# Attention with the causal mask of single-head score tiles added by VectorE instead of TensorE

## The reference

```python
att = jnp.einsum('bhqd,bhkd->bhqk', q, k) * scale
causal = jnp.tril(jnp.ones((T, T), bool))
att = jnp.where(causal[None, None], att, -jnp.inf)
y = jnp.einsum('bhqk,bhkd->bhqd', jax.nn.softmax(att, axis=-1), v)
qc, kc, vc = ...                     # the same heads against 64 context keys
y = y + jnp.einsum('bhqk,bhkd->bhqd', jax.nn.softmax(attc, axis=-1), vc)
```

## Time and profile before

| what | us |
|---|---|
| median of 3 runs | 2316.83 (2316.38 to 2319.52) |
| profiled execution, its own time | 2313.56 |
| its span | 2311.8 |
| PE busy | 2036.8 (88%) |
| DVE busy | 1556.2 (67%) |
| ACT busy | 1141.3 (49%) |
| POOL busy | 877.9 (38%) |

### The profile page before, as it was taken

How to read it: one execution, slowest core, us unless ns; L and a number is a source line. 1 busy time by engine, 2 the same in 40 slices (tenths; PEclk the granted TensorE clock), 3 DMA queues, 4 the chain that set the end, 5 groups by cost and what they waited for, 6 DMA issues and landing times. The chain is left out here.

```text
span 2311.8 us, 39759 instructions
## 1 busy us (share of the span) xinstructions
PE 2036.8 (88%) x12992; PEld 1413.1 (61%) x13056; DVE 1556.2 (67%) x2761; ACT 1141.3 (49%) x2247; POOL 877.9 (38%) x1276
## 2 busy tenths in 40 slices
PE   6786958999999975899999999999999999977998
PEld 5665846877777863555566556655566555535554
DVE  6897434555565444777877788777787777734776
ACT  6774234333434322365555555555555555554554
POOL 4444624444545432233343333433334333341332
PEclk9998979999999988999999999999999999997999
DMA  3443021122211125444333443334332443211222
GB/s 110 143 144 128 0 73 37 65 72 73 73 64 54 46 74 116 82 89 112 85 78 76 98 106 81 74 89 98 99 88 67 96 98 81 41 59 46 88 76 73
DMA packets 104479, 187.90 MB, mean 81 GB/s; under 512 B 27800, under 2 KB 77848, under 8 KB 98184
## 3 DMA queue, kind: packets, MB, share of 16 engines
q1 hardware_dynamic: 104328, 185.97, 29.9%
HBM read 110.07 MB, written 58.79 MB: 73 GB/s over the span
## 5 line engine op out<-in xcount | busy, mean ns | idle before, releaser
L1683 DVE TENSOR_REDUCE at_mneg<-at_ps_s 128x1 f32<-128x384 f32 (+3 forms) x704 | 437.8, 635 | 114.0 <-PE at_ps_s L1324 93.8
L1455 ACT ACTIVATE at_pt<-at_ps_w 128x512 f32<-128x512 f32 x640 | 375.1, 596 | 241.6 <-PE at_ps_w L1335 241.1
L1538 POOL TENSOR_SCALAR_AFFINE_SELECT at_pt<-at_pt 128x256 f32<-128x256 f32 (+1 forms) x640 | 230.6, 365 | 591.1 <-ACT at_pt L1455 588.5
L1323 PE MATMUL at_ps_s<-at_ks,at_qs 96*128 96x128 bf16 (+3 forms) x1024 | 258.3, 305 | 44.8 <-DVE at_mneg L1683 30.2
L1335 PE MATMUL at_ps_w<-at_qs,at_ks 97*128 97x512 bf16 (+3 forms) x1024 | 243.6, 300 | 8.5 <-ACT at_pt L1455 4.4
L1323 PEld LDWEIGHTS at_ps_s<-at_ks,at_qs 96*128 96x128 bf16 x1024 | 87.1, 99 | 236.0 <-DVE at_mneg L1683 135.9
L856 POOL TENSOR_TENSOR ml_m_lo<-ml_m,ml_m_hi 112x512 fp32r<-112x512 f32 x96 | 132.2, 1379 | 251.3 <-ACT ml_m_hi L784 251.2
L803 ACT ACTIVATE ml_gl<-ml_ps_g 112x512 f32<-112x512 f32 x96 | 57.4, 598 | 275.3 <-PE ml_ps_u L125 275.2
L1351 PE MATMUL at_ps_o<-at_pt,at_val 128*32 128x512 f32 (+3 forms) x2048 | 167.7, 446 | 9.3 <-POOL at_pt L1538 9.2
L1324 PE MATMUL at_ps_s<-at_mask,at_ident 128*128 128x128 bf16 (+1 forms) x640 | 148.1, 231 | 0.0
L1494 POOL TENSOR_TENSOR at_parts<-at_rest,at_parts 128x512 bf16<-128x512 f32 x64 | 74.4, 1162 | 157.0 <-ACT at_parts L1436 157.0
(11 more groups left out here) (235 smaller groups left out, 5615.3 us busy)
## 6 DMA issues: line engine op xcount, KB each, us to landing
parts_d<-at_parts SPq DMA_DIRECT2D x64, 384.0 KB, 2.5
at_ks<-parts_d SPq DMA_DIRECT2D x192, 128.0 KB, 7.4
at_qs<-parts_d SPq DMA_DIRECT2D x32, 384.0 KB, 4.9
pj_xin<-in_x SPq DMA_DIRECT2D x16, 512.0 KB, 5.1
gate_d<-pj_zc SPq DMA_DIRECT2D x16, 512.0 KB, 2.6
xv_all<-pj_turned_xv SPq DMA_DIRECT2D x16, 512.0 KB, 4.1
ml_turned_y<-xv_all SPq DMA_DIRECT2D x16, 512.0 KB, 3.4
ml_x<-gate_d SPq DMA_DIRECT2D x16, 512.0 KB, 4.3
```

Source lines behind the costliest of these rows:

```text
L1323: pe.matmul(out[:, i, :], qs[par][0:ROWS, h, toks], ks[par][0:ROWS, h, 0:(qt + 1) * P], start=i == 0, stop=False)
L1455: act.activation(pt[u % RING][:], ps_w[u % 2][:], ACT.Exp, scale=SCALE).then_inc(exped, 1)
L1538: pool.affine_select(out=diag, in_=diag, compare_op=ALU.is_ge, fill=0.0, base=0, pattern=pattern, channel_multiplier=-1).then_inc(cut, 1)
L1683: dve.tensor_reduce(mneg[:, g, h0 % HG:h0 % HG + count, qt], view_score(ps_s[s % 2], qt, count), AX_X, ALU.max, negate=True).then_inc(maxe ...
```

## The change

For tiles with one head (query tiles 2 and 3) TensorE no longer issues the mask product; the score product itself ends the tile and raises `scored`. VectorE replaces the negated maximum by one `tensor_tensor_reduce`: it reads the scores from PSUM and a bf16 mask from SBUF, adds them, multiplies by -1, writes the result back over the scores in PSUM, and gives the minimum of it (started from 3e38) into the same element of `mneg` through its accumulator output. For that, `mask16` becomes a row of 512 columns of which the last 128 hold the triangle and the others 0, and a tile of width w uses its last w columns. The tiles with two and four heads keep their mask product, which now reads the triangle broadcast over the heads. At the start of the block GpSimd makes the triangle in 128 columns instead of 512.

```diff
-        ... mask16 ... = ... n.sb("mask16", [P, HG, P], BF16) ...
+        ... mask16 ... = ... n.sb("mask16", [P, T], BF16) ...
@@ scores
+                own = count == 1
                 for i in range(count):
                     h = h0 + i
-                    pe.matmul(out[:, i, :], qs[par][0:ROWS, h, toks], ks[par][0:ROWS, h, 0:(qt + 1) * P], start=i == 0, stop=False)
-                pe.matmul(out[:, :, toks], ident16[:], mask16[:, 0:count, :], start=False, stop=True).then_inc(scored, 1)
+                    mm = pe.matmul(out[:, i, :], qs[par][0:ROWS, h, toks], ks[par][0:ROWS, h, 0:(qt + 1) * P], start=i == 0, stop=own)
+                if not own:
+                    mm = pe.matmul(out[:, :, toks], ident16[:],
+                                   mask16[:, T - P:T].unsqueeze(1).to_broadcast([P, count, P]), start=False, stop=True)
+                mm.then_inc(scored, 1)
@@ GpSimd, at the start of the block
-            pool.affine_select(out=mask16[:], in_=mask16[:], compare_op=ALU.is_ge, fill=-1e30, base=0,
-                               pattern=[[0, HG], [-1, P]], channel_multiplier=1).then_inc(const_set, 1)
+            pool.affine_select(out=mask16[:, T - P:T], in_=mask16[:, T - P:T], compare_op=ALU.is_ge, fill=-1e30, base=0,
+                               pattern=[[-1, P]], channel_multiplier=1).then_inc(const_set, 1)
@@ VectorE, step
-                            dve.tensor_reduce(mneg[:, g, h0 % HG:h0 % HG + count, qt], view_score(ps_s[s % 2], qt, count), AX_X, ALU.max,
-                                              negate=True).then_inc(maxed, 1)
+                            if count == 1:
+                                width = (qt + 1) * P
+                                dve.tensor_tensor_reduce(ps_s[s % 2][:, 0:width], ps_s[s % 2][:, 0:width], mask16[:, T - width:T], -1.0, 3e38,
+                                                         ALU.add, ALU.min, mneg[:, g, h0 % HG, qt:qt + 1]).then_inc(maxed, 1)
+                            else:
+                                dve.tensor_reduce(mneg[:, g, h0 % HG:h0 % HG + count, qt], view_score(ps_s[s % 2], qt, count), AX_X,
+                                                  ALU.max, negate=True).then_inc(maxed, 1)
```

More of the change, by code:

```diff
@@ L1052, in attend @@
         bias, bck, brow, xin, ctx2 = early.bias, early.bck, early.brow, early.xin, early.ctx2
-        ident16, mask16, ones = n.sb("ident16", [P, P], BF16), n.sb("mask16", [P, HG, P], BF16), n.sb("ones", [P, 64], BF16)
+        ident16, mask16, ones = n.sb("ident16", [P, P], BF16), n.sb("mask16", [P, T], BF16), n.sb("ones", [P, 64], BF16)
         x_hi, x_lo = n.sb("x_hi", [P, KT, T], F32R), n.sb("x_lo", [P, KT, T], F32R)
```

## The result

| | before | after |
|---|---|---|
| median, us | 2316.96 (2316.38 to 2319.52, 5 runs) | 2325.41 (2323.16 to 2329.5, 5 runs) |
| profiled execution: its own time, span | 2313.56, 2311.8 | 2323.93, 2322.2 |

The ratio is 1.0037, with a 95% interval of 1.0023 to 1.0052: slower by 0.4%. The prediction said 2327, and 2324.1 for the profiled execution.

A forecast was written before the change was run, and what follows sets the result against it. The prediction took the step as bound by PE and DVE in turn: 13 x 0.10 us added minus 10 x 0.06 us saved, +0.70 us over 15 steps, +10.5 us, giving 2327 us; 8-in-10 range 2307 to 2342.

The forecast's parts named there:

- The cut of the chain: One 72.94 us attention step split into eight parts by which engine sets the time; some 26 us run through DVE.
- The three PE stretches: Step parts from 1308.06, 1326.49 and 1349.34 us: 10 removed mask products at 0.06 us save 0.60 us per step.
- Maxima beside PE's stretches: The other 19 of 32 maxima per step, covered by DVE's waits; without cover, up to 1.9 us more per step.
- The price x: Extra DVE cost per new instruction: 0.10 us, from 0.01 data pass plus 0.09 read-out; ends 0 and 0.17 us.
- The three DVE stretches: Step parts from 1323.44, 1334.19 and 1361.87 us: 13 of 32 single-head maxima lie there, each 0.10 us dearer.
- stretch 5: 1334.19 to 1349.34 us of the step, DVE without waiting for another engine; five single-head maxima, forecast +0.50 us.
- stretch 7: 1361.87 to 1370.23 us of the step, bound by DVE; six single-head maxima, forecast +0.60 us.
- The sum: Per attention step 13 x 0.10 - 10 x 0.06 = +0.70 us; over 15 steps +10.5 us.
- the two terms cancel: Rival: a small read-out, 0.022 to 0.07 us extra per DVE instruction, within 4.6 us of before; chance 0.17.
- the three waits of PE: PE's waits for DVE at 1326.49, 1349.34 and 1370.23 us, forecast to grow because dearer maxima delay DVE's next work.
- Half rate: Rival: new DVE instruction takes two cycles per element, some 0.47 us extra, 2400 to 2543 us; chance 0.10 including anything above 0.17.
- GpSimd's shorter mask: At the block's start, hidden: the first score product waits 12.85 us for the DMA of the keys; no gain counted.

The follow-up runs named there:

- the placed change: The change made only in the 19 single-head tiles outside the DVE-bound parts of the step, against the kernel before: 2309.26 us, ratio 0.9963.
- VectorE's half alone: New VectorE operation kept, TensorE still issuing a same-size product with a mask of zeros, against the kernel before: 2324.3 us, ratio 1.0034.
- TensorE's half alone: Single-head mask products removed, VectorE keeping the plain maximum, those maxima unmasked, against the kernel before: 2307.3 us, ratio 0.9961.

## Why the prediction was right in its number and wrong in its reason

- **The cut of the chain** into PE's and DVE's stretches held. The three PE stretches gave -0.22, -0.13 and -0.24, together -0.59 us, where 10 x 0.06 = 0.60 was forecast; the placed change gave -0.66. Maxima beside PE's stretches cost nothing, as said.
- **The price x, the step that failed.** The prediction took 0.01 + 0.09 = 0.10 us from "the ScalarE row, the only one that shows the very thing". The 0.01 for the pass over the data was near (700 against 683 ns, 561 against 550), and so was 0 for the write to PSUM. The 0.09 for the read-out was not: on VectorE the next instruction starts with the read-out. The three DVE stretches grew by 0.02 + 0.11 + 0.21 = 0.34 us for 13 maxima, 0.026 us each instead of 0.10. Part of it is the 0.07 us by which the result comes later, once at the end of stretch 5 and once at the end of stretch 7, which the prediction had no term for. VectorE's half alone cost +0.37.
- The Trainium skill's "VectorE: DVE Perf Modes", section "Two Vector instructions with no wait between them", has an operation with accumulator output as two instructions. The trace agrees with it: 512 rows of each kind. The prediction leaned on it to carry the pattern of ScalarE over to VectorE, and took the size of the gap along with the pattern. Two rows in a profile are not two turns of the queue.
- **The sum.** +0.70 us a step was forecast, and the step without a fall went down by 0.28. x = 0.026 lies just inside the case "the two terms cancel", whose own range was 2312 to 2321 us, and below the break-even of 0.046. By the terms the prediction had, the time would have been 2316.8 - 15 x 0.28 = 2313 us.
- **The term that was missing.** The prediction said that the three waits of PE grow, and priced only the waits. It did not ask what TensorE's clock does behind a longer one. Seven falls among 13 steps cost 7 x 1.6 = 11.2 us, more than the change had saved, and by chance about what the wrong price had asked for. That the wait ahead of `n2` has a share in five of them is shown by filling it (these five gone), by moving the transpose (none left behind `n2`), and by making it longer in the kernel before (three falls appear). For the two behind `x_lo`, filling that wait took them away, but what brought them is not shown, since the wait had not grown.
- **Half rate** did not come: 700 ns for 512 columns. The upper end of this rival was also summed without the 0.60 us saved: 32 x 0.47 - 0.60 = 14.4 us a step makes +217 us, not +226.
- **GpSimd's shorter mask** shows no gain: the way to the first residual add got 1.76 us longer, with two falls more on it, so a small gain there could not be seen.
- **Open.** Why a wait of the same length is followed by a fall in one step and not in the next (1.67 to 1.69 us in each step of the change, falls behind it in five of 13), how much the missing products around it count (three falls against five for about the same wait), and why start and tail of the block lose some us in several of the kernels. The wait for `x_lo` is 1.17 us in before and 1.23 us with TensorE's half alone, both without a fall in the 13 steps; the change has two falls behind 1.19 us there. So the length of a wait alone does not decide, and no run separates what does.

## What to carry to other kernels

Price a new instruction by the distance of starts, and let a bound from another engine stay a bound: a duration of 140 ns may cost its queue nothing. Where a change lengthens a wait of TensorE, or takes work from around one, look at what follows the wait and at the granted clock there; a fall cost 1.6 us here, and seven of them undid a gain that every other row shows. A trade between two engines is best made tile by tile: take the work from the engine that is the bound at that place, and leave it where the other one is.

## What the runs showed of the hardware

- On VectorE the read-out of the accumulator (140 ns) overlaps with its neighbours: 0.61 us from the new operation to the next one, against 0.60 for a plain maximum; a second new operation right behind a read-out takes 0.65. On ScalarE the read-out took 0.09 us of the queue.
- An operation of VectorE that reads and writes the same PSUM tile and reads a bf16 row from SBUF takes 700 ns for 512 columns and 561 for 384, 17 and 11 ns more than a maximum that only reads.
- TensorE's granted clock fell from 1.00 to 0.50 behind waits of 1.19 and of 1.68 us, seven times in 13 steps, in a stage where PE is busy for nine tenths of the time (998 of 1100 us), and each fall cost 1.6 us. Behind other waits of the same lengths it did not fall. More products in such a wait, whose results nobody needed, made the kernel faster than the change (ratio 0.9956), though no faster than before.
